# Splitting the third stage's weights from the first step of the second stage on, and a tally that takes the last batch apart

## What is computed

```python
x = x + _L0_ffn_ref(_layernorm(x), ...)      # 8 experts, mixed by one share per expert for all tokens
x = x + _L1_xattn_ref(_layernorm(x), ctx, ctx, mask)   # one head, 256 wide: scores, softmax, weighted sum of ctx
def _L1_ffn_ref(x, W1, b1, W2, b2, Wg, bg):  # W1: 8 x 512 x 256, W2: 8 x 256 x 512
    w, idx = jax.lax.top_k(xt @ Wg.T + bg, 2)
    w = jax.nn.softmax(w, axis=1)
    y = relu(x @ W1.T + b1) @ W2.T + b2      # per expert
    return sum of the two chosen experts' y, weighted by w
```

## Time and profile before

| | |
|---|---|
| median of three runs | 1064.37 us |
| profiled execution | 1060.8 us, its span 1059.0 us |
| TensorE busy | 959.3 us (91%) |
| VectorE, ScalarE, GpSimd busy | 72%, 52%, 53% |
| DMA | 134 MB, mean 127 GB/s |
| second stage | from about 509.6 to 821.9 us of the span |

### The profile page before, as it was taken

One profiled execution on the slowest core, in us unless ns is written; L12 is line 12 of the kernel. 1 busy time (PEld: TensorE's weight loads), 2 busy tenths in 40 slices (PEclk: granted clock), 3 DMA queues, 4 the chain that ended last, 5 costly groups with the idle time before them and its releaser, 6 DMA issues. The chain is left out here.

```text
span 1059.0 us, 31414 instructions
## 1 busy us (share of the span) xinstructions
PE 959.3 (91%) x10666; PEld 675.3 (64%) x10666; DVE 763.2 (72%) x2164; ACT 552.9 (52%) x1090; POOL 564.6 (53%) x904
## 2 busy tenths in 40 slices
PE   4799999999999999988799999999963699999993
PEld 2466666666666666656456666666642588888872
DVE  4688788887888888894768888888765266666553
ACT  3566666666666666655224444444442355555541
POOL 6655454555545555410126777777776355555444
PEclk9999999999999999998799999999997799999997
DMA  5644344444444344322355656555561355555443
GB/s 153 174 136 135 104 121 122 136 110 123 118 127 136 110 122 120 108 79 83 104 151 166 187 189 194 181 179 184 182 197 58 119 91 90 98 96 92 83 63 41
DMA packets 104687, 134.03 MB, mean 127 GB/s; under 512 B 23713, under 2 KB 93873, under 8 KB 104369
## 3 DMA queue, kind: packets, MB, share of 16 engines
q1 hardware_dynamic: 90994, 113.93, 36.6%
q0 software_dynamic: 13536, 18.10, 10.1%
HBM read 93.80 MB, written 38.73 MB: 125 GB/s over the span
## 5 line engine op out<-in xcount | busy, mean ns | idle before, releaser
L991 DVE TENSOR_REDUCE smax<-psum 112x2 f32<-112x750 f32 x240 | 221.2, 934 | 45.8 <-PE psum L443 44.5
L823 ACT ACTIVATE probsT<-psum 125x896 f32<-125x896 f32 x173 | 158.8, 918 | 54.7 <-PE psum L458 53.4
L1963 POOL DMA_INDIRECT out_dram<-y,token_at x70 | 111.9, 1599 | 112.0 <-DMA out_dram<-y,token_at 53.5
L2044 ACT ACTIVATE h<-psum,b 128x256 f32<-128x256 f32 x140 | 58.7, 470 | 99.5 <-PE psum L1991 99.5
L1718 DVE SCALAR_TENSOR_TENSOR acc<-psum,neg_bias,acc 128x448 f32<-128x448 f32 x112 | 75.8, 679 | 10.8 <-PE psum L1542 10.7
L443 PE MATMUL psum<-k_stack,q_stack 63*128 63x375 f16 x480 | 78.5, 326 | 3.5 <-DVE smax L991 0.7
L478 PE MATMUL psum<-probsT,v_aug 125*32 125x112 f32 x2688 | 81.6, 262 | 0.0
L1461 POOL DMA_INDIRECT dispatch_dram<-rows,slots_at x64 | 64.0, 1000 | 28.4 <-issue 28.4
L1542 PE MATMUL psum<-xT_hi,we_hi 128*128 128x448 f16 x256 | 70.2, 356 | 1.1 <-ACT we_hi L1640 1.1
L396 POOL CAST k_hi<-we 128x375 f16<-128x375 f32 x64 | 31.9, 498 | 73.6 <-ACT we L843 73.5
L458 PE MATMUL psum<-q_stack,k_stack 64*128 64x112 f16 x1384 | 64.2, 212 | 7.3 <-DMA q_stack<-neg_max 2.7
(11 more groups left out here) (277 smaller groups left out, 2455.6 us busy)
## 6 DMA issues: line engine op xcount, KB each, us to landing
k_stack<-k_hi_dram SPq DMA_DIRECT2D x64, 188.0 KB, 2.8
we<-in_ctxT_dram SPq DMA_DIRECT2D x32, 375.0 KB, 3.7
ctxT<-in_ctxT_dram SPq DMA_DIRECT2D x32, 375.0 KB
ctx_rows<-in_ctx_dram SPq DMA_DIRECT2D x32, 375.0 KB
rows_e<-dispatch_dram SPq DMA_DIRECT2D x70, 136.0 KB, 2.4
w_raw<-in_w_dram SPq DMA_DIRECT2D x32, 256.0 KB, 3.8
k_hi_dram<-k_hi SPq DMA_DIRECT2D x32, 188.0 KB, 3.2
k_lo_dram<-k_lo SPq DMA_DIRECT2D x32, 188.0 KB, 3.4
```

The costliest lines, as they stand in the source:

```text
L823: nc.scalar.activation(probsT[:, p, c, hg, :, :, :].rearrange("p k h q -> p k (h q)"), psum[0:KC, 0:2, 0:4 * S], ACT.Exp, scale=float(HD) ...
L991: nc.vector.reduce_max(smax[:, (u - LAG_B) % 2, 2 * (s % 4) + s // 4::PAIRS], psum[0:S, pair_bank(s):pair_bank(s) + 2, 0:KV], AX.X).then_i ...
L1963: nc.gpsimd.indirect_dma_start(dram["out"], bass.IndirectOffsetOnAxis(token_at[:, n % 2, s:s + 1], 0), y[:, n % 2, s, :], None, compute_op ...
L2044: nc.scalar.activation(h[:, c, :], psum[:, 1 + c // 2, (c % 2) * TILE:(c % 2 + 1) * TILE], ACT.Relu, bias=b1[:, c, bass.ds(e, 1)]).then_in ...
```

## The change

Three things, in the code's words:

- The split of piece b moves on ScalarE and GpSimd from part a of step b+4 to part f of step b. It keeps its place among the other instructions of a step, so steps 0 to 3 get one, and steps 32 to 35 have none.
- On SP the load of the piece leaves `load` and becomes `load_weights`. Pieces 0 and 1 go out first, pieces 2 to 5 after the loads of batches 0 and 1, and from then on piece b+4 goes out behind the loads of batch b.
- The last batch isn't added to `cum` on GpSimd. TensorE sums `cum` (31 batches) and `chosen` (the last) in two matmuls into one result.

```diff
@@ SP
-            def load(t, u):
+            def load_weights(t, u):
                 b, p = t * TURN + u, u % 2
                 wait(sp, m["w_lo_rdy"], cnt(t, u - 2, 1, 1))
                 apart(sp)
                 sp.dma_start(w_raw[:, p, :], dram["w12"][:, bass.ds(b * W_PIECE, W_PIECE)]).then_inc(m[f"w_in{p}"], 16)
+            def load(t, u):
+                b, p = t * TURN + u, u % 2
                 wait(sp, m["s1_done"], cnt(t, u - 2, 1, 1))
...
             turns = B // TURN
+            for u in range(2):
+                load_weights(0, u)
             for u in range(TURN):
                 load(0, u)
+                if u == 1:
+                    for w in range(2, 2 + LAG_ATT):
+                        load_weights(0, w)
+                if u >= 2:
+                    load_weights(0, u + LAG_ATT)
                 if u >= 3:
                     store(0, u - 3)
             for t in range(1, turns):
                 for u in range(TURN):
                     load(t, u)
+                    if t * TURN + u + LAG_ATT < B:
+                        load_weights(t, u + LAG_ATT)
                     store(t, u - 3)
@@ GpSimd
-                if a:
-                    ua = u - LAG_ATT
-                    at = (t * TURN + ua) * W_PIECE
-                    wait(pool, m["w_hi_rdy"], cnt(t, ua, 1, 1))
+                if f:
+                    at = (t * TURN + u) * W_PIECE
+                    wait(pool, m["w_hi_rdy"], cnt(t, u, 1, 1))
...
+                if k and t * TURN + uk < B - 1:
                     wait(pool, m["cum_rdy"], cnt(t, uk - 1, 1, 1))
                     nc.gpsimd.tensor_tensor(cum[0:S, :], cum[0:S, :], chosen[:], ALU.add).then_inc(m["cum_rdy"], 1)
@@ TensorE
-            pe.wait_ge(m["cum_rdy"], B)
-            nc.tensor.matmul(psum[:, 0, 0:E], ones[0:S, :], cum[0:S, :], start=True, stop=True).then_inc(m["tally_done"], 1)
+            pe.wait_ge(m["cum_rdy"], B - 1)
+            pe.wait_ge(m["chosen_rdy"], B)
+            nc.tensor.matmul(psum[:, 0, 0:E], ones[0:S, :], cum[0:S, :], start=True, stop=False)
+            nc.tensor.matmul(psum[:, 0, 0:E], ones[0:S, :], chosen[:], start=False, stop=True).then_inc(m["tally_done"], 1)
@@ ScalarE
-                if a:
-                    wait(act, m[f"w_in{ua % 2}"], loads(t, ua))
+                if f:
+                    wait(act, m[f"w_in{u % 2}"], loads(t, u))
                     apart(act)
-                    nc.scalar.activation(w_hi[:, bass.ds((t * TURN + ua) * W_PIECE, W_PIECE)], w_raw[:, ua % 2, :], ACT.Copy).then_inc(m["w_hi_rdy"], 1)
+                    nc.scalar.activation(w_hi[:, bass.ds((t * TURN + u) * W_PIECE, W_PIECE)], w_raw[:, u % 2, :], ACT.Copy).then_inc(m["w_hi_rdy"], 1)
```

More of the change, by code:

```diff
@@ L1490, in step @@
                     scatter(t * TURN + u - LAG_SEND - 1)
-                if a:
-                    ua = u - LAG_ATT
-                    at = (t * TURN + ua) * W_PIECE
-                    wait(pool, m["w_hi_rdy"], cnt(t, ua, 1, 1))
+                if f:
+                    at = (t * TURN + u) * W_PIECE
+                    wait(pool, m["w_hi_rdy"], cnt(t, u, 1, 1))
                     apart(pool)
-                    nc.gpsimd.tensor_tensor(w_lo[:, bass.ds(at, W_PIECE)], w_raw[:, ua % 2, :], w_hi[:, bass.ds(at, W_PIECE)],
+                    nc.gpsimd.tensor_tensor(w_lo[:, bass.ds(at, W_PIECE)], w_raw[:, u % 2, :], w_hi[:, bass.ds(at, W_PIECE)],
                                             ALU.subtract).then_inc(m["w_lo_rdy"], 1)
```

## The result

The changed kernel takes 1118.03 us (median of six runs, 1115.12 to 1125.8) where six runs of the kernel before beside it took 1064.19 (1058.38 to 1065.72). The ratio taken over all runs, which isn't the quotient of these two medians (1.0506), is 1.0532, 95% interval 1.049 to 1.0574: slower, by 54 us on the medians. The profiled executions were 1117.64 and 1060.8 us, their spans 1115.9 and 1059.0, so 56.9 us are to be found in the trace (3.0 more than between the medians).

A forecast was written before the change was run, and what follows sets the result against it. TensorE was taken to bound the full steps at 8.47 us, a chain through all engines the drain. Loop + 29.9, start + 13.7 and drain - 1.6 made + 42.0 us: 1106.4 on the median, range 1076 to 1128.

The forecast's parts named there:

- the mechanism that was called likeliest: Full steps and start of the stage: both cost time, by late pieces; slower, 1106.4 us on the median, chance 0.70.
- Part 1: Full steps: the piece behind `ctx_rows` lands late, a closed loop makes steps 9.62 us, not 8.47; + 29.9 us over 26.
- Part 3: Drain: no `w_hi` or `w_lo` in steps 32 to 35 and a shorter tally gain time; - 1.6 us.
- 6.8 us from T to landing: Full steps: time from SP's issue of `ctx_rows` to the piece's landing, taken from the piece of step 5.
- T: Full steps: the moment SP issues `ctx_rows`; the piece behind it was forecast not before T + 0.39 us.
- the queue behind `ctx_rows`: Full steps: a piece issued behind `ctx_rows`, which holds about five DMA engines for 3.2 us, lands late.
- The bound of 5.65 us: Full steps: the loop is harmless if the piece lands sooner than this after the issue of `ctx_rows`; 8.47 - 2.82.
- Part 2: Start of the stage: five pieces through two buffers delay the first `x2n` by 11.9 us, plus 1.8 of clock; + 13.7 us.
- Only the start costs: Rival, full steps: the piece lands within 5.65 us, the loop doesn't bind, only the start costs; 1076.5 us, chance 0.13.
- The loop is worse: Rival, full steps: pieces take 7.4 us beside GpSimd's scatters, or TensorE's clock falls every step; 1125 to 1145, chance 0.09.
- Neither binds: Rival, whole stage: neither loop nor start costs, and the end gives its 1.6 us; 1062.8 us, chance 0.04.
- Faster: Rival, drain: its chain goes through GpSimd in all four steps, four `w_lo` and 2.3 us go; 1057.4 us, chance 0.04.

The follow-up runs named there:

- e6_store: The changed kernel with the store of x3 issued behind the mask of the next batch, not behind the piece: 1123.95 us, 1.0562.
- e1_ahead: The changed kernel with the piece issued between the mask and `ctx_rows` of a batch, no longer behind `ctx_rows`: 1077.42 us, 1.0131.
- e2_rows120: The changed kernel with `ctx_rows` loaded as two transfers of 120 and 5 partitions, the piece still behind both: 1072.99 us, 1.0079.
- e7_bufs4: e1_ahead with four buffers for the pieces in place of two, and another order of the first pieces: 1061.21 us, 0.998.
- e3_tally: The kernel before with only the change of the tally: 1062.64 us, 0.9987.
- e4_lag3: The kernel before with the tally change and pieces split three steps after their batch's first step, not four; loads keep their place: 1062.37 us, 0.9969.

## Why the prediction was right, and where it was off

1106.4 us and a range of 1076 to 1128 were forecast, 1118.03 was measured, by the mechanism that was called likeliest. In the traces + 42.0 us were forecast and + 56.9 measured; 12.6 of the difference are Part 1 and 2.4 are Part 3.

- **Part 1, the loop: mechanism right, size off.** + 29.9 forecast, + 42.5 in the trace. The part behind the landing was forecast at 2.82 us and is 10.11 - 7.3 = 2.8. The term that was mis-sized is "6.8 us from T to landing", which is 7.3 (0.39 and 6.9); 0.5 us x 26 = 13 us, nearly all of the miss. The row that I took, the only one with no store in between, fits the step that it stands for: 6.4 us there, 6.5 in step 5 of the changed kernel. What failed is that one row was put for all 26 steps. The two other rows would have been no better guide, since a store stands ahead of the piece in them and they landed at about T + 8.4 and T + 7.1. e6_store moved a store that stood behind the piece; it doesn't say what one ahead of it costs. Why the later pieces take longer is not settled. In the changed kernel those of steps 5 to 7 took 6.5, 6.8 and 6.7 us, those from step 8 on, when GpSimd's scatters begin, 6.9 by the mean, and 15 of these 23 took 6.8 to 7.2; in e6_store the first three took 6.3, 7.6 and 6.9. That fits a small part of the scatters and fits chance as well. Taking the scatters away wasn't tried, since the third stage addresses DRAM by what they write.
- **That the queue behind `ctx_rows` is what is late** was argued from the earlier trace rows and is now shown from both sides: by order (e1_ahead) and by engines (e2_rows120), each of which alone brings the step back to 8.47 to 8.49.
- **The bound of 5.65 us** was not reached by any landing in the changed kernel; e2_rows120 lands at T + 5.0 and doesn't pay. The runs put it between T + 5.0 and T + 7.3, no closer.
- **Part 2, the start.** + 13.7 forecast, 13.8 measured. By its parts: pieces 2 and 3 were split at 541.2 (541.5 forecast for the landing of piece 2), piece 4 at 546.1 (546.8), with a stage that began 0.5 us earlier; `x2n` came 11.6 us later against the stage's start (11.9). The clock: from `x2n` to the `ctx_rows` of step 5 it is 10.94 us in place of 8.80, so 2.1 for the 1.8 forecast. Some errors of 0.3 cancel. e7_bufs4 shows that all of it hangs on the late pieces: with them in time, neither the wait nor the clock is lost.
- **Part 3, the drain.** - 1.6 forecast, + 0.8 in the trace. The tally's share is there: - 1.0 us between the last logits and the third stage. The 0.19 us of the last `cum` GpSimd doesn't gain: its last scatter begins 0.86 us after its slots are ready in the kernel before, 0.87 in e3_tally. The wait that `w_lo` of piece 31 made is gone too. In the earlier trace rows `ln_var` starts 0.51 us after its `ln_mv` is there (0.80 in e3_tally); in the changed kernel, as in the six other kernels without that `w_lo`, it starts 0.19 or 0.20 after, and now waits for it:

```profile
858.96 0.18 DVE L1746 BATCH_NORM_AGGREGATE ln_mv<-ln_stats 112x2 f32<-112x6 f32 x1
859.33 0.22 POOL L1480 TENSOR_SCALAR ln_var<-ln_mv 112x1 f32<-112x1 f32 x1 [0.58 <-DVE ln_mv L1746]
```

From that `ln_mv` to the last logits the kernel before took 10.01 us at a mean clock of 0.86 (e3_tally 10.28 at 0.79), the changed one 9.71 at 0.84. So both gains can be seen, - 0.3 and - 1.0, within the bounds of the forecast (- 1.1 to - 2.8), though the smaller one rests on single traces. What undid them is ahead of that `ln_mv`: from the `ctx_rows` of step 31 to it the kernel before took 36.62 us at a mean clock of 0.91, the changed one 38.79 at 0.82, + 2.2. These 15 us of it, in the changed kernel, ran at about half clock:

```profile
834.00:849.00 15.00, 12.53 (x42) 8.21 (x43) 7.26 (x43) 5.25 (x13) 8.66 (x20) 0.54 0.41 121
```

Nothing shows that this is a cost of the change. e3_tally, whose code up to the last logits is that of the kernel before, took 37.96 us at 0.87 for the same stretch, so 1.3 us more with no cause in the code. Two kernels whose compute engines do the same in the drain, and whose SP differs only in where the stores go out and in `ctx_rows` in two parts, e6_store and e2_rows120, from the `ctx_rows` of step 31 to the third stage's first load:

```profile
823.83:881.12 57.29, 30.00 (x171) 20.32 (x168) 33.35 (x195) 17.22 (x44) 35.87 (x79) 0.81 0.35 109
```

```profile
772.43:833.60 61.17, 35.66 (x171) 23.85 (x168) 34.30 (x201) 17.84 (x45) 37.03 (x80) 0.72 0.36 102
```

3.9 us apart at clocks of 0.81 and 0.72, with 171 matmuls in both. A term of 0.3 to 0.5 us can't be seen in a total beside that. The step of Part 3 that failed is that it left the drain's clock as one trace had shown it.

- **The rivals.** "Only the start costs" (1076.5, chance 0.13) needs a landing within 5.65 us of T: e1_ahead made that case, and it took 1077.42. "The loop is worse" (1125 to 1145) has the right direction, but neither of its reasons held: pieces took 6.9 us beside the scatters and not 7.4, and the clock was 1.00 in all full steps with 1.4 us idle in each (262.77 - 225.71 = 37.1 over 26). "Neither binds" (1062.8) is what e4_lag3 and e7_bufs4 are, at 1062.37 and 1061.21. "Faster" (1057.4) needs a drain that hangs on GpSimd throughout; e7_bufs4 gave it every condition and stayed 3.8 us above.

## What to carry to other kernels

When a load moves in a queue, ask what stands directly ahead of it and on how many engines that one sits: `ctx_rows`, 375 KB over 125 partitions, made the piece behind it some 3 us later (6.9 against 4.1), and it cost nothing as long as the slow place was held by a store that no one waited for. A wait that closes a loop (o, then the load, then what o needs) costs in each step by how much the loop is longer than the bound, so a landing time that stands in such a sum 26 times needs bounds from more than the one row that looks cleanest. And a pipeline whose fill becomes deeper may need more buffers: with two for the five pieces ahead of the first consumer the start cost 7.9 to 13.9 us, by their order, with four and the order of e7_bufs4 0.1.

## What the runs showed of the hardware

- A load over 125 partitions kept the DMA share at 0.34 with 121 GB/s; cut in 120 and 5 partitions the same bytes ran at shares of 0.8 and more and 193 to 338 GB/s, for one more issue of 0.4 us on SP.
- A 256 KB piece took 6.9 us behind the first, 4.1 us behind the second, and 3.8 us in the place it had before, all by the median.
- Behind a stop of TensorE of 11.90 us its clock was at half until about 4.4 us after it began again. Five stops of 6.4 to 12.2 us cost 1.5 to 2.8 us each behind them (from `x2n` to the `ctx_rows` of step 5, less the 8.80 of the kernel before), and not by their length: the most behind 7.95 us (e2_rows120), the least behind 10.30 (e1_ahead). 1.4 us of idle time in each step of 10.1 us cost no clock at all.
- The drain, with TensorE busy for half of it, took 57.3 us at a mean clock of 0.81 and 61.2 us at 0.72 in two kernels with the same work on every compute engine. Changes of 1 us there are better read between two events behind the last clock change (here the last logits and the next stage's first load: 12.27 against 11.25 to 11.37 in eight kernels) than from a total.
